# Head projections of a linear attention: from float32 matmuls of head pairs to bf16 matmuls over exact pieces

## The chip, the cores and the metric

The kernel runs on one core of one Trainium2 chip. The metric is the device time of one execution in microseconds (us). The engines named here are TensorE (PE: matmuls; PEld: its weight loads), VectorE (DVE), ScalarE (ACT), GpSimd (POOL) and SyncE (SP), which issues all DMAs of this kernel.

## The reference, cut to what matters

A block of three layers over x of shape (16, 256, 128): an attention with random features, a small FFN with fp4-rounded weights and inputs, and a state-space mixer with an FFN behind it. The change touches only the projection inside the attention's features:

```
def _compute_features(z, omega, quad_nodes, quad_weights):     # z is q or k
    zn = z / jnp.maximum(jnp.linalg.norm(z, axis=-1, keepdims=True), 1e-12)
    proj = jnp.einsum('bhtd,rhdm->rbhtm', zn, omega)   # 16 heads, d = 8, 2 nodes x 32 features
    poly = proj ** 2 * inv_sqrt_m
    exp_arg = jnp.clip(proj * sqrt_2s - s, -20.0, 20.0)
    prf = jnp.exp(exp_arg) * inv_sqrt_m
    return poly * prf * sqw                            # 64 features a head
# attention: scores = qf . kf, causal, times v, divided by its own sum
```

Each head has 8 channels for q and 8 for k, and every token of every head gets 64 projected values.

## The kernel before

The 16 sequences are worked in 8 groups of 2 (512 tokens). The program is unrolled into 10 turns, and in turn i three groups are in flight: `new` (group i) is in attention, `mid` (group i-1) in the first FFN and the front of the mixer, `old` (group i-2) in the mixer's scan and the last FFN. Turn 0 has only `new`, turns 8 and 9 have none. Each turn is written for each engine as two loops of 16 slots, and every engine works its own list strictly in order, held only by semaphores:

- Loop A, slots k = 0 to 15. For `old`, one state of the scan a slot: ACT makes the decay (L716) and the drive (L728), PE turns the drive (L1476), DVE scans (L1159), POOL multiplies with a row of C (`read_out`, L624), PE adds the states up in PSUM (`sum_states`, L1492; state 14 at the end of the loop, state 15 after the first scores of loop B). For `new`: norm, qkv, the norm of each head, and at k = 12 and 13 on PE the turned q and k of sequence b = 0 and 1, into bank 3 of PSUM (L1587). For `mid`: the first FFN, its last matmuls (`down`) at k = 14.
- Loop B, slots 0 to 15, one slot for each pair of heads of each sequence of `new`: `project` (L1417), on ACT exp and square (L704, L707), on POOL a clip (L665; DVE does it for slots 0 to 2), on DVE the product of the two (`features`, L1148), on PE the scores (L1428, L1430), on DVE and ACT their masked copy (L1169, L737), on PE the context two slots later (L1454). Between them lie the mixer's front for `mid` and the last FFN for `old`.

The projection as it was: ACT copies bank 3 to `znt` (L822, float32, at k = 13 and 14), with all 16 heads x 8 channels on the 128 partitions. `omega` lies in SBUF as 128 x 8 pairs x 128, zero except in the rows of the pair's two heads, so one float32 matmul of 128 rows, 128 columns and 512 moving columns (q and k, 256 tokens each) gives the pair's 2 x 64 features in bank 0. The compiler makes two TensorE instructions of it. There is a single bank for it: `project(s)` waits for the square of slot s-1.

PE issues `project(0)` at k = 14 of loop A, `project(1)` at its end, `project(2)` in slot 0 of loop B and then `project(k + 2)` in slot k. The SP queue is in order too. In a turn it loads C rows 4 to 15 of `old` (each once its buffer is free), stores the C rows of `mid` to DRAM when ACT has written `xdbl` in loop B (`store_c`), loads the first four of them, and stores the output.

After loop A, POOL computes the deviation for the mixer's norm (L552 to L567), and ACT normalises with it (`xn_b`) behind the features of slots 0 and 1.

## Time and profile before

| | |
|---|---|
| median of 3 runs | 1375.67 us (1375.54 to 1377.26) |
| the profiled execution | 1378.12 us |
| its span, first to last instruction | 1376.4 us |
| mean granted TensorE clock | 0.910 |
| busy: PE, DVE, ACT, POOL | 82%, 72%, 68%, 35% of the span |
| matmuls of the projection | 256 instructions, 145.8 us of PE |
| first `project` of turns 0 to 4 | 33.0, 136.3, 276.0, 428.7, 580.2 us |
| last `project` | 1109.2 us |

The times in the timeline are from the span's start. Busy shares are shares of the whole span, and the turns differ: turn 0 has attention alone, turns 2 to 7 have everything, turns 8 and 9 have no attention. A granted clock of 1.00 is 2.4 GHz, 0.50 is 1.2 GHz.

### The profile page before, as it was taken

The page shows a single profiled execution, that of the slowest core. Times are in us where ns is not written, and L with a number is a line of the kernel's source. Part 1 is how long each engine was busy: PE and PEld are TensorE (multiplying, and loading weights), DVE is VectorE, ACT ScalarE, POOL GpSimd, SP SyncE. Part 2 cuts the span into 40 slices and gives each one's busy share as a digit, 9 for nine tenths or more (in the row PEclk, how much of TensorE's full clock was granted, in tenths as well). Part 3 has the DMA queues.
Part 4 walks back from the last instruction along what each step waited for, and adds up shares of the span by engine and source line. Part 5 has one row for each costly group of instructions (what it writes and reads, how often), then busy time and mean ns, then how long its engine had stood idle before and what let it go on. Part 6 is the DMA issues. An engine that isn't in the chain of part 4 may idle for free. (4 is left out here: it accounts for less than half of the span.)

```text
span 1376.4 us, 17231 instructions
## 1 busy us (share of the span) xinstructions
PE 1126.2 (82%) x5421; PEld 621.8 (45%) x5421; DVE 985.4 (72%) x1472; ACT 937.2 (68%) x1829; POOL 484.4 (35%) x457
## 2 busy tenths in 40 slices
PE   3875887899789988899789988999889987747844
PEld 1343344544544454545544454545544454415423
DVE  1645559886897689876897689877897688645733
ACT  3543779677885769576885869586886768467711
POOL 3110216531454116621454126511543126405623
PEclk8986899999999999999999999999999999967865
DMA  2000002100110002100120102100110002001200
GB/s 73 1 8 0 19 14 62 39 1 32 41 60 9 32 1 77 31 2 31 46 54 8 33 10 68 31 24 10 48 53 1 32 24 61 17 31 38 62 0 8
DMA packets 31403, 41.12 MB, mean 30 GB/s; under 512 B 4617, under 2 KB 14674, under 8 KB 31314
## 3 DMA queue, kind: packets, MB, share of 16 engines
q1 hardware_dynamic: 31314, 40.02, 10.0%
q8 instruction: 46, 0.75, 0.2%
q14 instruction: 43, 0.35, 0.1%
HBM read 37.65 MB, written 2.36 MB: 29 GB/s over the span
## 5 line engine op out<-in xcount | busy, mean ns | idle before, releaser
L624 POOL TENSOR_TENSOR read<-state,c_row 128x1024 f32<-128x1024 f32 x128 | 300.4, 2358 | 237.7 <-DVE state L1159 68.5
L1159 DVE TENSOR_TENSOR_SCAN state<-decay,bank 128x512 f32<-128x512 f32 x256 | 295.7, 1203 | 57.5 <-PE bank L1476 48.0
L1492 PE MATMUL bank<-read,ident 128*128 128x512 f32 x512 | 258.7, 634 | 1.1 <-POOL read L624 1.1
L1476 PE MATMUL bank<-ident,drive_by_token 128*128 128x128 f32 x1024 | 161.6, 294 | 95.7 <-DVE state L1159 85.6
L728 ACT ACTIVATE drive_by_token<-dtu_t,b_t 128x256 f32<-128x256 f32 x512 | 217.3, 500 | 1.0 <-PE bank L1476 0.9
L665 POOL TENSOR_SCALAR expf<-expf 128x512 f32<-128x512 f32 x104 | 69.2, 665 | 379.6 <-ACT expf L704 379.0
L1476 PEld LDWEIGHTS bank<-ident,drive_by_token 128*128 128x128 f32 x1024 | 119.5, 148 | 162.3 <-issue 104.8
L716 ACT ACTIVATE decay<-dt,neg_a 128x510 f32<-128x510 f32 x256 | 169.7, 714 | 16.4 <-DVE state L1159 16.3
L1169 DVE TENSOR_TENSOR s_sb<-bank,causal 128x512 f32<-128x512 f32 x128 | 88.2, 689 | 112.5 <-PE bank L1430 112.5
L1417 PE MATMUL bank<-znt,omega 128*128 128x512 f32 x256 | 145.8, 653 | 10.2 <-ACT sqf L707 10.2
L704 ACT ACTIVATE expf<-bank,minus_s,root2s 128x512 f32<-128x512 f32 x128 | 99.3, 776 | 69.2 <-PE bank L1417 66.0
L1492 PEld LDWEIGHTS bank<-read,ident 128*128 128x128 f32 x512 | 97.8, 208 | 86.1 <-issue 80.1
L1454 PE MATMUL bank<-s_sb,vext 128*32 128x256 f32 (+1 forms) x1024 | 130.7, 344 | 3.2 <-ACT s_sb L737 2.9
L1428 PE MATMUL bank<-feat 64*128 64x256 f32 x512 | 96.0, 439 | 12.5 <-ACT s_sb L737 11.8
L737 ACT ACTIVATE s_sb<-bank 128x256 f32<-128x256 f32 x128 | 48.8, 381 | 76.7 <-DVE s_sb L1169 76.5
L1148 DVE SCALAR_TENSOR_TENSOR feat<-expf,scale_f,sqf 128x512 f32<-128x512 f32 x128 | 95.3, 744 | 7.0 <-POOL expf L665 4.4
L1454 PEld LDWEIGHTS bank<-s_sb,vext 128*32 128x32 f32 x1024 | 39.7, 109 | 98.4 <-issue 62.0
L1428 PEld LDWEIGHTS bank<-feat 64*128 64x128 f32 x512 | 43.6, 192 | 75.8 <-issue 61.5
L707 ACT ACTIVATE sqf<-bank 128x512 f32<-128x512 f32 x128 | 75.5, 589 | 0.0
L1417 PEld LDWEIGHTS bank<-znt,omega 128*128 128x128 f32 x256 | 44.8, 202 | 47.2 <-issue 42.1
L1430 PEld LDWEIGHTS bank<-feat 64*128 64x128 f32 x512 | 55.7, 193 | 4.1
L1430 PE MATMUL bank<-feat 64*128 64x128 f32 x512 | 54.4, 276 | 0.0
(236 smaller groups left out, 1694.6 us busy)
## 6 DMA issues: line engine op xcount, KB each, us to landing
c_row<-c_rows SPq DMA_DIRECT2D x128, 256.0 KB, 3.2
xa<-x_dram SPq DMA_DIRECT2D x8, 256.0 KB, 3.6
out_dram<-x SPq DMA_DIRECT2D x8, 256.0 KB, 2.3
omega<-omega_t_dram SPq DMA_DIRECT2D x1, 512.0 KB
c_rows<-xdbl SPq DMA_DIRECT2D x8, 32.0 KB, 1.6
wqkv<-w_qkv_t_dram SPq DMA_DIRECT2D x1, 192.0 KB
state<-w_down_dram SPq DMA_DIRECT2D x1, 176.0 KB, 2.5
state<-w_gate_dram SPq DMA_DIRECT2D x1, 128.0 KB, 2.0
```

The lines of the kernel that those rows point to most:

```text
L624: pool.tensor_tensor(read[:, s % STATE_BUFFERS], state[:, s % STATE_BUFFERS], c_row[:, s % C_BUFFERS].unsqueeze(1).broadcast_to([P, DT, TO ...
L704: act.activation(expf[:, s % 2], bank[:, 0], ACT.Exp, bias=minus_s[:], scale=root2s[:]).then_inc(exp_done.sem, 1)
L716: last = act.activation(decay[:, s % 2, k, :, 1:], dt[:, k].rearrange("p (b t) -> p b t", b=SEQS)[:, :, 1:], ACT.Exp, scale=neg_a[:, k, s: ...
L728: last = act.activation(by_token[:, s % DRIVES, t], dtu_t[:, t], ACT.Identity, scale=b_t[:, t, s:s + 1])
L1148: dve.scalar_tensor_tensor(feat[:, s % 2], expf[:, s % 2], scale_f[:], sqf[:, s % 2], ALU.mult, ALU.mult).then_inc(feat_done.sem, 1)
L1159: dve.tensor_tensor_scan(state[:, s % STATE_BUFFERS, c], decay[:, s % 2, c].rearrange("p b t -> p (b t)"), bank[:, DRIVE_BANK + c], 0.0, A ...
L1417: pe.matmul(bank[:, 0], omega[:, j], znt[:, b], start=True, stop=True).then_inc(proj_ps.sem, 1)
L1428: pe.matmul(bank[:, 1 + h, 0:SEQ], f[:, SEQ:SEQ + P], f[:, 0:SEQ], start=True, stop=True)
L1430: last = pe.matmul(bank[:, 1 + h, SEQ:SEQ + P], f[:, SEQ + P:], f[:, P:SEQ], start=True, stop=True)
L1454: last = pe.matmul(o, columns, scored, start=(k == 0 and below == 0), stop=(k == 1 and below == 1))
L1476: last = pe.transpose(bank[:, DRIVE_BANK + c, t * P:(t + 1) * P], by_token[:, s % DRIVES, t, c * P:(c + 1) * P], ident[:])
L1492: last = pe.matmul(bank[:, 6 + k], ident[:], read[:, s % STATE_BUFFERS, k], start=(s == 0), stop=(s == STATES - 1))
```

## The change

Each float32 value of z and of omega is split into three bf16 values (high, middle, low) whose sum is the value. The product of a head is then the sum of nine products of 8 channels, and these are stacked on 3 x 3 x 8 = 72 rows of one bf16 matmul: rows (i, d, j) hold piece i of z and piece j of omega. So a slot has two matmuls, one a head, each of 72 rows, 64 columns and 512 moving columns, into the lower and the upper half of bank 0.

What is new for each sequence: ACT writes the high piece from bank 3 (in the place of the copy to `znt`), DVE subtracts it (`z_left`), ACT rounds that to the middle piece (one slot later, so behind the high piece of the other sequence), POOL subtracts again and has the low piece (`z_lowest`, before `read_out` of slots 14 and 15). SP stores the three pieces to DRAM and loads, for each head, the 24 rows of it, each repeated on three partitions; a slot has one of 4 buffers. DVE splits omega in turn 0 (five operations on 72 x 1024), and it also goes through DRAM once. `project(0)` and `project(1)` now stand at the end of loop A, behind the sum of state 14. Some pairs of semaphores were merged, with the same order of work.

```
+            def store_z(group, b):
+                for i, piece in enumerate((z_high, z_mid, z_low)):
+                    sp.wait_ge(piece.sem, piece.at(group, b + 1))
+                    sp.dma_start(z_dram[b, :, i], z_part[:, b, i]).then_inc(z_stored.sem, 16)
+            def load_z(group, s):
+                b, j = divmod(s, PAIRS)
+                sp.wait_ge(z_stored.sem, z_stored.at(group, PIECES * (b + 1)))
+                sp.wait_ge(proj_ps.sem, proj_ps.at(group, s + 1 - Z_BUFFERS))
+                for half, h in enumerate(heads_of(j)):
+                    sp.dma_start(
+                        z_row[:, s % Z_BUFFERS, half],
+                        z_dram[b, h].rearrange("i d t -> (i d) t").unsqueeze(1).broadcast_to(
+                            [PIECES * HD, PIECES, 2 * SEQ])).then_inc(
+                                z_loaded[s % Z_BUFFERS].sem, 16)
...
+                if turn.has_new:
+                    store_z(turn.new, 0)
+                    for s in range(Z_BUFFERS):
+                        load_z(turn.new, s)
+                    store_z(turn.new, 1)
+                    for s in range(Z_BUFFERS, 12):
+                        load_z(turn.new, s)
                 if turn.has_mid:
                     store_c(turn.mid)
                     for s in range(C_BUFFERS):
                         load_c(turn.mid, s)
+                if turn.has_new:
+                    for s in range(12, SLOTS):
+                        load_z(turn.new, s)
...
+            def z_lowest(group, b):
+                pool.wait_ge(z_mid.sem, z_mid.at(group, b + 1))
+                pool.tensor_tensor(z_part[:, b, 2], z_left[:], z_part[:, b, 1], ALU.subtract
+                                   ).then_inc(z_low.sem, 1)
             def body(turn):
                 for k in range(SLOTS):
+                    if turn.has_new and k in (14, 15):
+                        z_lowest(turn.new, k - 14)
                     attention_rest(turn, k)
                     if turn.has_old:
                         read_out(turn, k)
...
                     act.wait_ge(znt_ps.sem, znt_ps.at(new, b + 1))
-                    act.activation(
-                        znt[:, b], bank[:, 3].rearrange("p (k t) -> p k t", k=2), ACT.Copy
-                    ).then_inc(znt_done.sem, 1)
+                    act.wait_ge(z_stored.sem, z_stored.at(new, PIECES * (b + 1 - SEQS)))
+                    act.activation(z_part[:, b, 0], bank[:, 3], ACT.Copy).then_inc(z_high.sem, 1)
+                if turn.has_new and k in (14, 15):
+                    b = k - 14
+                    act.wait_ge(z_rest.sem, z_rest.at(new, b + 1))
+                    act.activation(z_part[:, b, 1], z_left[:], ACT.Copy).then_inc(z_mid.sem, 1)
...
+                if turn.is_first and k == 1:
+                    split_omega()
+                if turn.has_new and k in (13, 14):
+                    b = k - 13
+                    dve.wait_ge(z_high.sem, z_high.at(new, b + 1))
+                    dve.wait_ge(z_low.sem, z_low.at(new, b))
+                    dve.tensor_tensor(z_left[:], bank[:, 3], z_part[:, b, 0], ALU.subtract
+                                      ).then_inc(z_rest.sem, 1)
...
             def project(ga, s):
-                b, j = divmod(s, PAIRS)
-                pe.wait_ge(znt_done.sem, znt_done.at(ga, b + 1))
+                loaded_row = z_loaded[s % Z_BUFFERS]
+                pe.wait_ge(loaded_row.sem, loaded_row.at(ga, 2 * (s // Z_BUFFERS + 1)))
                 pe.wait_ge(sq_done.sem, sq_done.at(ga, s))
-                pe.matmul(bank[:, 0], omega[:, j], znt[:, b], start=True, stop=True).then_inc(
-                    proj_ps.sem, 1)
+                for half, h in enumerate(heads_of(s % PAIRS)):
+                    last = pe.matmul(bank[PH * half:PH * (half + 1), 0], omega[:, h],
+                                     z_row[:, s % Z_BUFFERS, half], start=True, stop=True)
+                last.then_inc(proj_ps.sem, 1)
...
-                    pe.wait_ge(znt_done.sem, znt_done.at(new, b))
+                    pe.wait_ge(z_rest.sem, z_rest.at(new, b))
...
                     if turn.has_mid and k == 14:
+                        if turn.has_new:
+                            pe.wait_ge(z_rest.sem, z_rest.at(new, SEQS))
                         down(ffn_a, mid, 1)
-                    if turn.has_new and k == 14:
-                        project(new, 0)
                     if turn.has_old:
                         for s in SUMS[k]:
                             sum_states(old, s)
                     attention_rest(turn, k)
-                if turn.has_new:
-                    project(new, 1)
                 if turn.has_old:
                     sum_states(old, STATES - 2)
+                if turn.is_first:
+                    pe.wait_ge(omega_moved, 32)
+                if turn.has_new:
+                    project(new, 0)
+                    project(new, 1)
```

## Rows read from the trace of the kernel before

**Rows 1.** Groups of instructions: busy us, mean ns of one, idle before it.

```profile
L1417 PE MATMUL bank<-znt,omega 128*128 128x512 f32 x256 | 145.8, 653 | 10.2 <-ACT sqf L707 10.2
...
L704 ACT ACTIVATE expf<-bank,minus_s,root2s 128x512 f32<-128x512 f32 x128 | 99.3, 776 | 69.2 <-PE bank L1417 66.0
...
L1169 DVE TENSOR_TENSOR s_sb<-bank,causal 128x512 f32<-128x512 f32 x128 | 88.2, 689 | 112.5 <-PE bank L1430 112.5
...
L707 ACT ACTIVATE sqf<-bank 128x512 f32<-128x512 f32 x128 | 75.5, 589 | 0.0
```

**Rows 2.** Windows of turn 4, loop B; PE, PEld, DVE, ACT, POOL busy (instructions), clock, DMA.

```profile
595.00:618.00 23.00, 21.95 (x115) 9.73 (x114) 20.36 (x39) 19.05 (x36) 4.67 (x9) 0.99 0.01 2
618.00:648.00 30.00, 28.41 (x152) 14.71 (x150) 18.88 (x27) 20.60 (x35) 4.25 (x6) 0.89 0.12 36
```

**Rows 3.** The same two windows, the instructions of the projection (L1417) alone: PE, PEld.

```profile
595.00:618.00 23.00, 5.32 (x10) 1.66 (x10) 0.99 0.01 2
618.00:648.00 30.00, 7.20 (x12) 2.28 (x12) 0.89 0.12 36
```

**Rows 4.** Timeline of PE, a slot of loop B in turn 4: start, us.

```profile
605.12 1.02 PE L1417 MATMUL bank<-znt,omega 128*128 128x512 f32 x2
606.08 0.62 PE L1454 MATMUL bank<-s_sb,vext 128*32 128x256 f32 x4
606.63 0.71 PE L1428 MATMUL bank<-feat 64*128 64x256 f32 x4
...
607.84 1.12 PE L1417 MATMUL bank<-znt,omega 128*128 128x512 f32 x2
```

**Rows 5.** Timeline of PE between loop A and loop B in turn 4.

```profile
576.56 0.60 PE L1587 MATMUL bank<-ident,qk 128*128 128x128 f32 x4
...
580.21 1.02 PE L1417 MATMUL bank<-znt,omega 128*128 128x512 f32 x2
...
585.45 0.71 PE L1428 MATMUL bank<-feat 64*128 64x256 f32 x4
...
588.68 0.63 PE L1409 MATMUL bank<-ident,xn_b 128*128 128x128 f32 x4 [0.38 <-ACT xn_b L692]
```

**Rows 6.** Timeline of POOL over the same stretch.

```profile
570.56 6.96 POOL L624 TENSOR_TENSOR read<-state,c_row 128x1024 f32<-128x1024 f32 x3 [2.83 <-DVE a_ffn_h L1127]
580.79 2.35 POOL L624 TENSOR_TENSOR read<-state,c_row 128x1024 f32<-128x1024 f32 x1 [3.27 <-DVE state L1159]
...
586.50 0.35 POOL L567 TENSOR_TENSOR b_ln_shift<-b_ln_shift,b_ln_rstd 128x4 f32<-128x4 f32 x2
```

**Rows 7.** Timeline of turn 0, all engines.

```profile
24.00 1.26 POOL L641 TENSOR_TENSOR xab<-xa,bout 128x512 f32<-128x512 f32 x1 [11.92 <-DMA wglu<-glu_w_t_dram]
...
30.22 1.08 PE L1587 MATMUL bank<-ident,qk 128*128 128x128 f32 x4 [8.77 <-DVE qk L1231]
31.34 0.60 ACT L822 ACTIVATE znt<-bank 128x512 f32<-128x512 f32 x1 [4.03 <-PE bank L1587]
...
32.97 1.92 PE L1417 MATMUL bank<-znt,omega 128*128 128x512 f32 x2
```

**Rows 8.** DMA issues: count, KB each, us from issue to landing.

```profile
c_row<-c_rows SPq DMA_DIRECT2D x128, 256.0 KB, 3.2
...
c_rows<-xdbl SPq DMA_DIRECT2D x8, 32.0 KB, 1.6
```

**Rows 9.** Timeline of the SP queue: start, us of the issue.

```profile
16.70 0.43 SPq L455 DMA_DIRECT2D wmix<-mix_out_t_dram  x1
```

**Rows 10.** Windows of turns 0 and 1, loop B, columns as in rows 2.

```profile
33.00:90.00 57.00, 49.49 (x306) 23.72 (x305) 33.18 (x54) 29.18 (x56) 8.79 (x13) 0.93 0.01 1
136.00:206.00 70.00, 61.18 (x346) 29.20 (x346) 37.97 (x63) 50.37 (x95) 11.93 (x20) 0.92 0.06 16
```

**Rows 11.** Windows of turn 4 where the granted clock falls, columns as in rows 2.

```profile
612.00:618.00 6.00, 4.95 (x27) 2.17 (x26) 5.86 (x11) 4.35 (x11) 0.96 (x2) 0.97 0.03 7
618.00:624.00 6.00, 6.00 (x16) 2.30 (x16) 0.67 (x1) 4.48 (x9) 0.61 (x1) 0.50 0.56 175
```

More of the change, by code:

```diff
@@ L39 @@
 CROWS, CTILE, CPITCH = 16, 32, 48
+PIECES = 3
+ROWS = PIECES * PIECES * HD
+Z_BUFFERS = 4
 CHUNKS = SEQ // P
@@ L137, in build @@
         bout = sb("bout", [P, C])
-        omega = sb("omega", [P, PAIRS, P])
+        omega = sb("omega_pieces", [ROWS, HEADS, PH], BF16)
         node = sb("node", [P, 1])
@@ L175, in build @@
         vext = sb("vext", [P, TILES, HEADS, CPITCH])
-        znt = sb("znt", [P, SEQS, 2, SEQ])
+        z_part = sb("z_pieces", [P, SEQS, PIECES, 2 * SEQ], BF16)
+        z_row = sb("z_rows", [ROWS, Z_BUFFERS, 2, 2 * SEQ], BF16)
         expf = sb("expf", [P, 2, 2 * SEQ])
@@ L183, in build @@
         ctx_t = sb("ctx_t", [P, 2 * SEQ])
+        z_left = ctx_t
+        omega_all = feat[0:ROWS].rearrange("p k t -> p (k t)")
+        omega_left = expf[0:ROWS].rearrange("p k t -> p (k t)")
+        omega_part = s_sb[0:ROWS].rearrange("p k h t -> p (k h t)")[
+            :, 0:PIECES * HEADS * PH // 2].bitcast(BF16).rearrange(
+                "p (i c) -> p i c", i=PIECES)
         rden = sb("rden", [P, CHUNKS * HEADS])
@@ L341, in build @@
         znt_ps = events("a_znt_in_psum", SEQS)
-        znt_done = events("a_znt", SEQS)
+        z_high = events("a_z_high", SEQS)
+        z_rest = events("a_z_rest", SEQS)
+        z_mid = events("a_z_mid", SEQS)
+        z_low = events("a_z_low", SEQS)
+        z_stored = events("a_z_in_dram", SEQS * PIECES, 16)
+        z_loaded = [events(f"a_z_rows_{j}", 2 * SLOTS // Z_BUFFERS, 16) for j in range(Z_BUFFERS)]
         proj_ps = events("a_proj_in_psum", SLOTS)
@@ L428, in _ @@
             sp.dma_start(wqkv[:], w_qkv_t).then_inc(attention_loaded, 16)
[L429 removed]
+            sp.dma_start(bqkv, b_qkv).then_inc(attention_loaded, 16)
             sp.dma_start(node[:], nodes).then_inc(attention_loaded, 16)
             sp.dma_start(scale_f[:], weights).then_inc(attention_loaded, 16)
[L432 removed]
+            sp.dma_start(omega_all, omega_t).then_inc(attention_loaded, 16)
             for e in every_event:
@@ L548, in deviation @@
             def deviation(norm, group):
-                pool.wait_ge(norm.var.sem, norm.var.at(group, 1))
+                pool.wait_ge(norm.var.sem, norm.var.at(group, 2))
                 mean, var = norm.mean_var[:, :, 0], norm.mean_var[:, :, 1]
@@ L689, in normalise @@
             def normalise(norm, group, src, dst, layer=0):
-                act.wait_ge(norm.dev.sem, norm.dev.at(group, 1))
+                act.wait_ge(norm.dev.sem, norm.dev.at(group, 3))
                 for t in range(TILES):
@@ L767, in h_magic @@
                 act.activation(f.quant_h.magic, f.h[pair][:].rearrange("p t n -> p (t n)"),
-                               ACT.Abs, scale=LIFT).then_inc(f.h_magic.sem, 1)
+                               ACT.Abs, scale=LIFT).then_inc(f.magic.sem, 1)
             def ffn_ht(f, group, pair):
@@ L1024, in statistics @@
                     last = dve.bn_stats(norm.stats[:, t], src[:, t])
-                last.then_inc(norm.counted.sem, 1)
-                dve.wait_ge(norm.counted.sem, norm.counted.at(group, 1))
+                last.then_inc(norm.var.sem, 1)
+                dve.wait_ge(norm.var.sem, norm.var.at(group, 1))
                 for t in range(TILES):
@@ L1116, in hidden_lifted @@
             def hidden_lifted(f, group, pair):
-                dve.wait_ge(f.h_magic.sem, f.h_magic.at(group, pair + 1))
+                dve.wait_ge(f.magic.sem, f.magic.at(group, pair + 2))
                 lift(f.quant_h, hidden(f, pair)).then_inc(f.h_lifted.sem, 1)
@@ L1403, in _ @@
             pe.matmul(bank[:, 7, 0:3 * C], minus_part[:], wqkv[:], start=True, stop=False)
-            pe.matmul(bank[:, 7, 0:3 * C], part[:], bqkv[:], start=False, stop=True
+            pe.matmul(bank[:, 7, 0:3 * C], part[:], bqkv, start=False, stop=True
                       ).then_inc(bias_spread, 1)
@@ L1813, in head_pairs @@
         t = omega.transpose(1, 2, 0, 3).reshape(HEADS, HD, PH)
-        laid = np.zeros((HEADS, HD, PAIRS, 2, PH), omega.dtype)
-        for j in range(PAIRS):
-            for half, h in enumerate(heads_of(j)):
-                laid[h, :, j, half] = t[h]
-        return laid.reshape(HEADS * HD, PAIRS, 2 * PH)
+        rows = np.repeat(t.transpose(1, 0, 2).reshape(HD, HEADS * PH), PIECES, axis=0)
+        return np.tile(rows, (PIECES, 1))
     def columns(v):
```

52 lines of the change are left out of this document (35 added, 17 removed).

## The prediction

> **What bounds the kernel now.** I read the groups of instructions first, then the timelines of one slot and of the place between the loops, then the windows. The reader is to see in the groups that the projection is 256 TensorE instructions of 0.65 us, and that ACT has 0.78 + 0.59 us of exp and square behind each pair of them [rows 1]. The timeline of a slot shows the pace: after a projection starts, the context starts 0.96 us later, and the next projection after 2.72 us, with no idle mark on any PE line; PE is the engine that this slot waits for [rows 4]. The windows say how long this holds in turn 4, one of the six full turns (2 to 7). From 595 to 618 us PE is busy 21.95 of 23 us, but DVE 20.36 and ACT 19.05 too: three engines are near their limit. From 618 to 648 PE has 28.41 of 30, DVE only 18.88 and ACT 20.60: there PE alone sets the pace [rows 2]. The projection is 5 pairs of instructions (5.32 us) of the first and 6 pairs (7.20 us) of the second [rows 3]. Turns 0 and 1 are the clearest case, PE 49.49 of 57 and 61.18 of 70 us [rows 10]. So a cheaper projection pays in loop B, by less than its own busy time.
>
> Between the loops another chain counts. POOL finishes the product of state 15 at 583.14, works out the deviation until 586.85 [rows 6], and PE can turn the normalised tiles only at 588.68 [rows 5]. Whatever delays POOL's last two products delays the mixer's front of that turn.
>
> **The price of the new matmul.** No bf16 matmul is in the trace. From above: two instructions at the price of the two float32 ones, 0.96 us, a gain of nothing; from below 0. The nearest row is the context: four instructions of 256 columns on different column tiles, two heads, take 0.55 us (606.08 to 606.63) [rows 4]. Two of 512 columns on two column halves stream as many columns. That would be 0.55 us; since a float32 instruction does more work a column than a bf16 one should, I take 0.5, which saves 0.5 us a slot of PE (0.96 to 1.05 before).
>
> The Trainium skill ("TensorE: Matmul & The Clock Gate", "Back-to-back issue gap") puts a bf16 matmul of 512 columns at 216 ns from start to start at the full clock, and its part on row and column tiling lets column tiles run at once: an estimate of 0.43 us or of some 0.22 for the pair. By the first the total below would be about 2 us lower; the second is the first rival. No run here shows it yet.
>
> **What it brings in loop B of a full turn.** 595 to 618: 5 x 0.5 = 2.5 us of PE, but DVE leaves only 23 - 20.36 = 2.64 us, and part of that waits on ACT and POOL; I credit half, 1.3. 618 to 648: 6 x 0.5, plus 0.5 because one of the six runs at the half clock (7.20 us for six against 5.32 for five, so about 1.9 for that one [rows 3]), 3.5 us, and DVE has 11 us free: 3.3. The other three of the fourteen stand in the ramp and the tail: 1.5 us, of which I credit 0.9. Sum 5.5 us.
>
> **What it costs between the loops, full turn.** I follow turn 4. PE turns sequence 1 at 576.56, done 577.16 [rows 5]. The high piece of sequence 1 (ACT 0.6, as the copy to `znt` [rows 7]) ends at 577.8, and only behind it, in ACT's order, comes the middle piece of sequence 0, to 578.4. `z_lowest(0)` on POOL then: nearest is the 128x512 addition of 1.26 us [rows 7], above it half a `read_out` (6.96 / 3 / 2 = 1.16) [rows 6]; I take 1.2, to 579.6. Queued behind it is `read_out(14)`, which ended at 577.5 before; now it runs 579.6 to 581.95. `z_lowest(1)` follows to 583.15, then `read_out(15)` to 585.5 instead of 583.14: 2.35 us late. The deviation, the normalisation and the tiles at 588.68 come as much later, about 591.0. DVE: `z_left` of sequence 1 waits for POOL's 579.6 and takes 0.69 (the mask, also read from PSUM [rows 1]), so the scan of state 15 ends near 582.6, before POOL wants it. PE's `down` waits for that 580.3; 1.5 us idle. The extra DVE 2 x 0.7 and ACT 2 x 0.6 us lie in waits of these engines here.
>
> Does the data reach `project(0)`? The low piece is there at 579.6. A store of 128 KB is between the 32 KB that landed after 1.6 us and the 256 KB after 3.2 [rows 8]; the loads of 72 KB likewise, two of them, 0.43 us apart on SP [rows 9]. With 2.0 and 2.0 the row is there at 584.1, before PE has summed state 14 (about 585.4). `project(0)` is then 5 us later than the 580.21 of before, but the scores, at 585.45 before, come at 585.4 + 0.5 + 0.8 exp + 0.5 clip + 0.75 product = 588.1 or so: 2.65 us late and near the same delay, and the transposes of `xn_b` follow at 591.0. The cost is 2.35 us.
>
> PE now has several idle pieces of 1 to 1.5 us in a place that was full. The granted clock fell after a stretch with PE at 4.95 of 6 us, and the next 6 us ran at 0.50 [rows 11]. I count half of such a stretch more, 3 us at 1.2 GHz, at 1 us of path.
>
> Full turn: 2.35 + 1 - 5.5 = -2.15 us, times six -12.9.
>
> **Turns 0 and 1.** Turn 1: 15 x 0.5 = 7.5 us, times PE's share 61.18 / 70 [rows 10], 6.5; the entry costs 2, the clock 1: -3.5. Turn 0 has nothing to hide the round trip. The first copy ends at 31.94 [rows 7]; then `z_left` 0.7, PE's second transposes 1.1, high 0.6, middle 0.6, low 1.26, store 2.0, second load 0.43 + 1.6: `project(0)` at about 40.3 instead of 32.97, +7.3. Its slots save 14 x 0.5 = 7, but DVE rounds weights in nine of them (33.18 of 57 us busy in all [rows 10]); I credit 5.5. Net +1.8. Splitting omega (five operations, 5 to 6 us of DVE) lies between the norm and the sums of squares, where DVE waits, and its round trip ends long before 40 us.
>
> **SP.** In loop B each slot issues two loads, 0.86 us of SP, and a row may be loaded when the projection four slots earlier is done, 11 us at 2.72 a slot, against 0.43 + 3.2 at worst. `store_c` stands behind the load for slot 11, which needs `project(7)`, issued before `xdbl` is made; the four C rows (1 MB) then go ahead of slot 12's row, with some three slots in hand. Cost nothing; if that cover is gone, slots 12 to 15 wait.
>
> **Sum.** -12.9 - 3.5 + 1.8 = -14.6 us. The profiled execution took 1378.12 us, 1.72 around its span of 1376.4; it would be 1363.5. Against the median 1375.67 it gives 1361.
>
> **The rivals.**
> - PE is the whole pace and the halves overlap (pair 0.25, saving 0.75): 14 x 0.75 = 10.5, credited 9.5, less 2.35, is -7.2 a full turn, -43; turns 0 and 1 -2 and -9. About 1322. For it: no idle on PE lines in the slot [rows 4]. Against: DVE at 20.36 of 23 [rows 2].
> - DVE and ACT set the pace as soon as PE gives way: only the stretch from 618 pays, 2.4 us, which the entry takes: about 1376. For it: the same 20.36 and 19.05.
> - The granted clock, and this one ends slower. The projection was the densest work of the slot, 128 x 128 tiles; what stays are the context's and the scores' small tiles, and PE idles more. Where PE was at 4.95 of 6 us the clock fell to 0.50 for the next 6 [rows 11]. If each loop B has 10 us more of that, PE does 5 us less work in it, times eight is +40: 1361 + 40 = 1401. It decides from 14.6 / 8 = 1.8 us a turn, 3.7 us more at 1.2 GHz. Against: turn 0 keeps a mean of 0.93 [rows 10]. The Trainium skill ("TensorE: Matmul & The Clock Gate", on how the clock gate oscillates) has the clock follow how busy PE has been; rows 11 agree in so far as the fall comes behind idle pieces, but PE was at 83% there.
> - The pair costs what the float32 pair did, 0.96: nothing is saved, and 6 x 3.35 + 3 + 7.3 = +30: 1406. Slower, too.
> - The rows come late. With 3.2 us a transfer [rows 8] `project(0)` moves 2.4 us, less 1.3 in hand; with PE at the entry late by about 2 us in each of eight turns, 1377.
>
> **How the numbers follow.** Chances: forecast 0.43 (1348 to 1373), overlap 0.13, DVE and ACT 0.14, clock 0.18, no cheaper 0.05, late rows 0.07. Faster by over 0.2% (2.8 us, about what a measurement of this kernel can tell from no change): 0.43 + 0.13, and 0.03 each of the second and third rival, 0.62. Same: 0.06 of the second, 0.02 of late rows, 0.08. Slower: 0.30. The range from 1320 to 1398 leaves out the last two hundredths of the overlap, the no-cheaper case and half of the clock case, together 0.16 to 0.2.
>
> **What the profile after would show.** Right: the two instructions of the projection 0.2 to 0.3 us apart, the slot's pace in turn 0 down from 2.8 towards 2.3 us; POOL's `read_out` of state 15 2.4 us behind the transposes of sequence 1 compared with before; turns 2 to 7 some 2 us shorter; `project(0)` of turn 0 near 40 us, released by a DMA. Wrong: a mean clock under 0.88; idle of PE in front of the projection put down to DMA in slots above 4; a projection that keeps PE for 0.9 us; DVE over 90% in loop B with PE at 75%. The most fragile terms are the credits of rows 2 and the clock.

## The result, and the profile after

The changed kernel took 1398.9 us (median of 4, 1396.6 to 1409.28) against 1376.47 of the kernel before in the same session: a ratio of 1.0172 (95%: 1.0117 to 1.0227). It is 1.7% slower; 1361 was forecast, 1398 was the top of the range. The profiled execution is the slowest of the four (1409.28, 10 us above their median), so its pieces add up to more than the median's difference. The granted clock is the first thing to see, the new kernel above the old one:

```profile
core 0: 1407.5 us, clock 0.872
```

```profile
core 0: 1376.4 us, clock 0.910
```

The clock has two levels, 1.2 and 2.4 GHz, so a mean of 0.872 says that 1407.5 x 2 x 0.128 = 360 us ran at 1.2 GHz, against 248 before. The three unprofiled runs had 0.876 to 0.880. The prediction had named a mean clock under 0.88 as a sign of being wrong. The groups of instructions of after, to read beside [rows 1], say that the matmul itself became at least as cheap as forecast:

```profile
L1506 PE MATMUL bank<-z_rows,omega_pieces 72*64 72x512 bf16 x256 | 57.2, 437 | 38.8 <-ACT sqf L767 28.4
...
L1518 PE MATMUL bank<-feat 64*128 64x256 f32 x512 | 108.5, 477 | 27.8 <-ACT s_sb L797 24.3
```

PE's time in the projection fell from 145.8 to 57.2 us. It now waits 38.8 us in front of it (10.2 before), mostly for the square on ACT, which frees bank 0. A slot of loop B in turn 4, PE's timeline, against [rows 4]:

```profile
622.12 0.41 PE L1506 MATMUL bank<-z_rows,omega_pieces 72*64 72x512 bf16 x2
622.45 0.63 PE L1544 MATMUL bank<-s_sb,vext 128*32 128x256 f32 x4
623.01 0.71 PE L1518 MATMUL bank<-feat 64*128 64x256 f32 x4
...
624.82 0.41 PE L1506 MATMUL bank<-z_rows,omega_pieces 72*64 72x512 bf16 x2 [0.54 <-ACT sqf L767]
```

The context follows 0.33 us after the projection instead of 0.96: 0.63 us saved. But the last line starts only after an idle 0.54 us.

I cut both traces at the first transposes of `att` of each turn. The whole difference between the two profiled executions (31 us) can be placed with that:

| us | before | after | forecast of the difference | measured |
|---|---|---|---|---|
| turn 0 | 90.2 | 93.5 | +1.8 | +3.3 |
| turn 1 | 116.3 | 116.9 | -3.5 | +0.6 |
| turns 2 to 7 | 920.9 | 947.1 | -12.9 | +26.2 |
| the rest | 249 | 250 | 0 | +1 |

These are the marks themselves, before and then after: the ends of turns 0, 1 and 7.

```profile
90.25 0.66 PE L1409 MATMUL bank<-ident,att 128*128 128x128 f32 x4 [1.13 <-DVE att L1184]
...
206.54 0.66 PE L1409 MATMUL bank<-ident,att 128*128 128x128 f32 x4 [0.26 <-DVE att L1184]
...
1127.48 0.60 PE L1409 MATMUL bank<-ident,att 128*128 128x128 f32 x4
```

```profile
93.52 0.65 PE L1497 MATMUL bank<-ident,att 128*128 128x128 f32 x4 [1.13 <-DVE att L1263]
...
210.45 0.66 PE L1497 MATMUL bank<-ident,att 128*128 128x128 f32 x4 [0.26 <-DVE att L1263]
...
1157.54 0.60 PE L1497 MATMUL bank<-ident,att 128*128 128x128 f32 x4
```

Inside the full turns, loop A gave back 0.7 us a turn and the entry (from the first transposes of q and k to the mixer's first projection, `xp`) took 3.8 us more on average. Loop B, which was to give 5.5 us, gave nothing and took 1.3 us more on average: 75.2 to 78.1 us, where before had 73.7 to 76.9. In turn 4, from `xp` to the transposes, windows of before and after (columns as in [rows 2]):

```profile
590.20:667.00 76.80, 70.63 (x394) 37.68 (x395) 56.59 (x98) 56.45 (x104) 10.66 (x20) 0.93 0.05 15
```

```profile
608.60:684.60 76.00, 67.67 (x394) 37.52 (x395) 55.52 (x96) 56.42 (x104) 10.63 (x17) 0.87 0.12 36
...
629.00:642.00 13.00, 11.17 (x46) 5.44 (x48) 6.63 (x12) 9.66 (x20) 1.89 (x3) 0.61 0.34 103
```

PE has 3 us less work, counted at a lower clock: 0.87 against 0.93. The last line is 13 us out of it at 0.61, with PE busy 86% of the time.

### The profile page after: what moved, and what is told of

Read it like the earlier page. It is cut to its first block and busy times, and to the rows that moved or that the text cites. A ratio compares the mean times of both kernels' runs of the same rounds, so it can differ in the third digit from the quotient of the medians.

```text
span 1407.5 us, 17744 instructions
## 1 busy us (share of the span) xinstructions
PE 1096.2 (78%) x5421; PEld 621.4 (44%) x5421; DVE 991.3 (70%) x1493; ACT 943.4 (67%) x1845; POOL 502.4 (36%) x473
## 5 line engine op out<-in xcount | busy, mean ns | idle before, releaser
L1544 PE MATMUL bank<-s_sb,vext 128*32 128x256 f32 (+1 forms) x1024 | 142.7, 374 | 1.8 <-ACT s_sb L797 0.9
L1518 PE MATMUL bank<-feat 64*128 64x256 f32 x512 | 108.5, 477 | 27.8 <-ACT s_sb L797 24.3
L1518 PEld LDWEIGHTS bank<-feat 64*128 64x128 f32 x512 | 50.5, 208 | 87.3 <-issue 73.3
L1506 PE MATMUL bank<-z_rows,omega_pieces 72*64 72x512 bf16 x256 | 57.2, 437 | 38.8 <-ACT sqf L767 28.4
L1520 PEld LDWEIGHTS bank<-feat 64*128 64x128 f32 x512 | 65.8, 216 | 5.0
L1544 PEld LDWEIGHTS bank<-s_sb,vext 128*32 128x32 f32 x1024 | 42.7, 116 | 52.4 <-issue 35.1
L1520 PE MATMUL bank<-feat 64*128 64x128 f32 x512 | 63.1, 300 | 0.0
L1506 PEld LDWEIGHTS bank<-z_rows,omega_pieces 72*64 72x64 bf16 x256 | 15.7, 110 | 96.6 <-issue 75.1
```

What stands on the lines that cost most here:

```text
L1518: pe.matmul(bank[:, 1 + h, 0:SEQ], f[:, SEQ:SEQ + P], f[:, 0:SEQ], start=True, stop=True)
L1520: last = pe.matmul(bank[:, 1 + h, SEQ:SEQ + P], f[:, SEQ + P:], f[:, P:SEQ], start=True, stop=True)
L1544: last = pe.matmul(o, columns, scored, start=(k == 0 and below == 0), stop=(k == 1 and below == 1))
```

## The experiments

"Ratio" is to the kernel before on the same chip. The time at 1.2 GHz is 2 x time x (1 - clock), the mean over the runs of a kernel.

| kernel | ratio (95%) | median us | us at 1.2 GHz |
|---|---|---|---|
| before | 1 | 1373.0 to 1377.2 | 238 to 246 |
| after | 1.0172 (1.0117 to 1.0227) | 1398.9 | 345 |
| e1_one_piece | 1.0022 (0.9992 to 1.0052) | 1375.58 | 328 |
| e2_filler | 1.0352 (1.0301 to 1.0402) | 1424.48 | 276 |
| e3_late_float32 | 1.0043 (1.0009 to 1.0076) | 1380.0 | 231 |
| e4_two_buffers | 1.0208 (1.016 to 1.0255) | 1403.43 | 354 |
| e5_no_dram | 1.0001 (0.9967 to 1.0035) | 1373.25 | 285 |
| e6_one_piece_warm | 0.9903 (0.987 to 0.9937) | 1360.46 | 250 |
| e7_one_piece_light | 0.9787 (0.9758 to 0.9815) | 1344.72 | 290 |
| e8_before_light | 0.9939 (0.991 to 0.9967) | 1367.33 | 240 |
| e9_warm | 1.0077 (1.0047 to 1.0107) | 1385.05 | 262 |
| e10_three_products | 0.9894 (0.9875 to 0.9914) | 1361.06 | 245 |
| e11_traffic | 1.0011 (0.9987 to 1.0035) | 1377.64 | 291 |
| e12_traffic_waited | 1.0030 (0.9996 to 1.0063) | 1381.86 | 295 |
| e13_wide | 1.0196 (1.017 to 1.0222) | 1404.86 | 330 |
| e14_column_halves | 1.0039 (1.0011 to 1.0067) | 1382.44 | 296 |
| e15_72_rows | 1.0146 (1.0095 to 1.0197) | 1393.45 | 330 |
| e16_128_rows | 1.0047 (1.0021 to 1.0073) | 1382.28 | 294 |

(A single run of e11_traffic of 1938 us, at a clock of 1.0, stands outside its ratio and its mean. What made it is not known.)

**e1_one_piece.** Before, with the cheap matmul alone, at its old place:

```
+        omega_b = sb("omega_bf16", [P, PAIRS, P], BF16)
-        znt = sb("znt", [P, SEQS, 2, SEQ])
+        znt = sb("znt", [P, SEQS, 2, SEQ], BF16)
...
-                pe.matmul(bank[:, 0], omega[:, j], znt[:, b], start=True, stop=True).then_inc(
+                pe.matmul(bank[:, 0], omega_b[:, j], znt[:, b], start=True, stop=True).then_inc(
```

> The kernel before with only the matmul made cheap: znt and omega rounded once to bf16 (so the projection has bf16 precision, the two lower pieces and seven of the nine products are left out), one 128x128x512 bf16 matmul a slot in the old places, no DMA, no pieces. If PE sets the pace of loop B, some 0.7 us x 14 slots x 8 turns come off less a part: 1320 to 1345. If DVE and ACT take over the pace at once, 1370 to 1378 with the mean granted clock at about 0.91. If the clock takes it back, loop B gets more stretches at 0.50, the mean clock falls below 0.89, and the time is 1365 to 1385.

1.0022: the price of the projection can fall with nothing else changed, and the kernel doesn't get faster. What was lost isn't only in the entry. The clock fell from 0.910 to 0.885:

```profile
core 0: 1367.8 us, clock 0.885
```

**e2_filler.** After, with useless float32 work in front of each pair, to bring PE's load back:

```
             def project(ga, s):
...
+                pe.matmul(bank[:, 0, 0:3 * C], ident[:], wqkv[:], start=True, stop=True)
```

> The changed kernel with a float32 matmul of 384 columns (0.7 us) put in front of each pair, into the same bank, its result overwritten: PE has its old load back. If PE sets the pace at a full clock, 0.7 us x 14 x 8 x 0.7 is +55 us: 1450. If DVE and ACT set it, within 5 us of the 1399 of the changed kernel or up to 20 above. If the clock took the gain, the fillers restore it: mean clock over 0.90, and the time at 1399 or below it.

It was far too much work, and it stands in turns 0 and 1 too (103.6 and 129.1 us against 93.5 and 116.9). 1.0352 doesn't decide between the theories by itself. But the time at 1.2 GHz fell from 345 to 276 us, and the six full turns took 943.5 us with 96 fillers of 384 columns in them, against the 947.1 of the profiled after. That run of after was 10 us above its median and this one 3, so the fillers cost a few us there and not nothing; but it is little for so much work, and it asked for the finer dose of e6 and e9.

**e3_late_float32.** Before, with `project(0)` and `project(1)` at the late place:

```
-                    if turn.has_new and k == 14:
-                        project(new, 0)
...
-                if turn.has_new:
-                    project(new, 1)
                 if turn.has_old:
                     sum_states(old, STATES - 2)
...
+                if turn.has_new:
+                    project(new, 0)
+                    project(new, 1)
```

> The kernel before with only project(0) and project(1) moved behind the sum of state 14, float32 as they were. If the entry costs by its order alone, it is slower by 2 to 4 us in each of seven turns: 1390 to 1405. If the entry's cost comes from POOL's two subtractions and the clock, within 5 us of before, for the deviation on POOL still ends last.

1.0043: the later place costs about 0.4%, 6 us, and by itself lowers no clock (231 us at 1.2 GHz).

**e4_two_buffers.** After, with a `z_left` for each sequence, so that nothing of DVE waits for POOL's first subtraction, and both subtractions behind `read_out(14)`:

```
-        z_left = ctx_t
+        z_left = feat
...
-                    if turn.has_new and k in (14, 15):
-                        z_lowest(turn.new, k - 14)
+                    if turn.has_new and k == 15:
+                        z_lowest(turn.new, 0)
+                        z_lowest(turn.new, 1)
...
-                    dve.wait_ge(z_low.sem, z_low.at(new, b))
...
+                    dve.wait_ge(z_low.sem, z_low.at(turn.new, SEQS))
```

> The changed kernel with a buffer of z_left for each sequence (in the idle feature buffers), so that DVE doesn't wait for POOL before the scan of state 15, and with both low pieces behind read_out(14). If the entry costs by the wait of DVE and POOL's order, about 2 us in each full turn come back: 1383 to 1389. If the entry's cost is the late rows and the clock, under 4 us: 1395 to 1399.

1.0208, no faster than after. The deviation is ready 2.1 us sooner in turn 4: POOL's last product of it now ends 9.7 us after the second transposes of q and k started (591.86), 11.8 in after. But the next wait was right behind, the row out of DRAM (PE, then POOL):

```profile
600.31 0.41 PE L1507 MATMUL bank<-z_rows,omega_pieces 72*64 72x512 bf16 x2 [0.84 <-DMA z_rows<-z_in_dram]
...
601.24 0.35 POOL L619 TENSOR_TENSOR b_ln_shift<-b_ln_shift,b_ln_rstd 128x4 f32<-128x4 f32 x2
```

ACT normalises only behind the features of slots 0 and 1. In turn 4 the entry still became 2.1 us shorter, but over the six full turns it averages 23.9 us against 24.1 in after, so what POOL gained did not last. The order on POOL, to which the prediction gave the whole price of the entry but for 1 us, isn't alone in it.

**e5_no_dram.** After, with the chain of pieces on ACT, DVE and POOL and the late place kept, but no transfers, and one matmul over the high pieces where they lie:

```
-                loaded_row = z_loaded[s % Z_BUFFERS]
-                pe.wait_ge(loaded_row.sem, loaded_row.at(ga, 2 * (s // Z_BUFFERS + 1)))
+                b, j = divmod(s, PAIRS)
+                pe.wait_ge(z_low.sem, z_low.at(ga, b + 1))
...
+                pe.matmul(bank[:, 0], omega_b[:, j], z_part[:, b, 0], start=True, stop=True).then_inc(
+                    proj_ps.sem, 1)
```

> The changed kernel without its DMAs of z and omega: the pieces are made as they are, but the projection is one bf16 matmul of the high pieces of a pair (128 x 128), at the end of loop A, so seven of nine products are left out. If the round trip through DRAM sets the entry, 2 us or more a turn come back and turn 0 is 5 us shorter: 1380 or less. If POOL's order and the clock set it, 1390 to 1399 but for turn 0.

1.0001. The 1.7% goes with what e5 took away: the traffic and its waits, or the shape of the matmul.

**e6_one_piece_warm.** e1 with useless float32 work of 256 columns before the projections from slot 3 on, in turns with `old`:

```
+                if warm:
+                    pe.matmul(bank[:, 0, 0:256], ident[:], wqkv[:, 0:256], start=True, stop=True)
```

> The one-piece kernel with a float32 matmul of 256 columns (0.5 us) in front of each projection from slot 3 on in turns 2 to 9. Turns 0 and 1 and all entries keep their cheap matmul. If the clock takes the gain of the cheap matmul in the full turns, this work costs nothing: loop B (from the first matmul of the mixer to the next turn's first transposes) stays at 73 to 76 us and the granted clock in it rises to over 0.95. If the cheap matmul's time is needed, loop B gets longer by 13 x 0.5 x 0.7 = 4 us or more in each full turn, +25 in all.

0.9903 against the 1.0022 of e1, with disjoint intervals. More work on PE, a higher clock, a shorter kernel:

```profile
core 0: 1364.9 us, clock 0.905
```

**e7_one_piece_light and e8_before_light.** e1, and before, with exp, square and the product cut to 256 of 512 columns:

```
-                act.activation(sqf[:, s % 2], bank[:, 0], ACT.Square).then_inc(sq_done.sem, 1)
+                act.activation(sqf[:, s % 2, 0:SEQ], bank[:, 0, 0:SEQ], ACT.Square).then_inc(sq_done.sem, 1)
```

> The one-piece kernel with exp, square and their product on 256 of the 512 columns (the other half of the features isn't computed), so ACT does some 0.54 us and DVE some 0.3 us less in each slot. If these two engines and the chain from projection through exp and square set the pace of loop B once PE gives way, 14 x 0.5 x 6 and more come off: 1320 to 1340. If PE's clock is what holds it, little changes, under 10 us.

> The kernel before with the same halves left out. If PE alone set the pace before, nothing changes: 1366 to 1376. If ACT and DVE were already part of the pace, it gains as much as the one-piece kernel does from the same cut.

The same cut is worth 2.35% behind the cheap matmul and 0.6% in before, so ACT and DVE hold the kernel more once PE gives way. Loop B of the full turns says the same when it is compared at an equal granted clock: with light features it took 73.1 us against 73.7 to 74.1 in before (clock 0.98), and 72.2 to 72.8 against 74.4 to 74.9 in e1 (clock 0.91). That the six full turns as a whole took 903.8 us in e7 and 904.2 in e8 fits with the clock: 290 us at 1.2 GHz against 240.

**e9_warm.** After with fillers as in e6, and two more between the loops:

```
+                            pe.matmul(bank[:, 2, 0:HID], ident[:], wqkv[:, 0:HID], start=True,
+                                      stop=True)
...
+                    if turn.has_mid:
+                        pe.matmul(bank[:, 1, 0:3 * C], ident[:], wqkv[:], start=True, stop=True)
...
-                            project(new, k + 2)
+                            project(new, k + 2, turn.has_old)
```

> The changed kernel, whole, with useless float32 matmuls: 256 columns (0.5 us) in front of the pair from slot 3 on in turns 2 to 9, 352 columns where PE waits for z_left at the end of loop A, 384 between project(0) and project(1). If the clock's theory holds for the changed kernel as it did for the one-piece one (-1.2%), 1375 to 1388, with a mean clock over 0.89. If the changed kernel is held by its rows and not by the clock, the added work costs 0 to 20 us: 1399 to 1420.

1.0077 against 1.0172, with disjoint intervals too: over half of the loss came back by adding work.

```profile
core 0: 1382.3 us, clock 0.907
```

**e10_three_products.** High and middle pieces only, three of the nine products. The pieces stay where ACT and DVE write them (128 rows), three accumulating matmuls a slot, at the old places, no POOL step and no transfer:

```
+                pe.matmul(bank[:, 0], omega_b[:, 1, j], znt[:, b, 0], start=True, stop=False)
+                pe.matmul(bank[:, 0], omega_b[:, 0, j], znt[:, b, 1], start=False, stop=False)
+                pe.matmul(bank[:, 0], omega_b[:, 0, j], znt[:, b, 0], start=False, stop=True).then_inc(
```

> Another way to the cheap projection: high and middle piece of z and of omega stay in SBUF in the old 128-row layout, and three bf16 matmuls of 128x128x512 (high x high, high x middle, middle x high) add up in bank 0, in the old places; the smaller products are left out. No DMA, one subtraction on DVE a sequence. PE has some 0.65 us a slot, between the one-piece kernel and before. If the clock is kept by dense work, as with the filler, it is faster than before by 0.5 to 1%: 1360 to 1368. If only float32 work keeps it, as the one-piece kernel: 1370 to 1380.

0.9894: faster than both kernels. It has three matmuls where e1 has one, and its ratio is 1.3% lower, with 245 us at 1.2 GHz instead of 328. It differs from e1 in one subtraction a sequence as well, which can only cost. PE in turn 4:

```profile
601.63 0.39 PE L1429 MATMUL bank<-znt,omega_bf 128*128 128x512 bf16 x1
601.86 0.38 PE L1430 MATMUL bank<-znt,omega_bf 128*128 128x512 bf16 x1
602.07 0.38 PE L1431 MATMUL bank<-znt,omega_bf 128*128 128x512 bf16 x1
602.38 0.63 PE L1468 MATMUL bank<-s_sb,vext 128*32 128x256 f32 x4
```

0.75 us from the first to the context, against 0.96 of float32 and 0.33 of after.

**e11_traffic and e12_traffic_waited.** e5 with all stores and loads running again; in e12 each projection also waits for its row, though it doesn't read it:

```
+                loaded_row = z_loaded[s % Z_BUFFERS]
+                pe.wait_ge(loaded_row.sem, loaded_row.at(ga, 2 * (s // Z_BUFFERS + 1)))
```

> The kernel without DRAM in the path (high pieces only, one matmul a slot), but the stores and loads of the z rows run as in the changed kernel; nothing but SP waits for them. If the traffic itself costs (SP's issues, C rows delayed, contention), it goes from 1.000 of before towards 1.017. If only the waiting for the rows costs, it stays at 1.000 of before, within 0.3%.

> The run before (traffic, high pieces only, one 128x128 matmul a slot) with one thing more: each projection waits until its rows have been loaded, as in the changed kernel; it doesn't read them. What is left between it and the changed kernel is the form of the matmul (two of 72 rows and 64 columns). If the waiting for rows costs the 1.6% between them, it comes to 1.013 to 1.019 of before. If the small tiles do, by the clock, it stays below 1.005.

1.0011 and 1.0030. Against e5 the traffic comes to 0.1% and the wait to 0.2% more, with errors of some 0.4% each, so neither can be told from nothing. The profiled runs show where the wait lies: turn 0 took 87.6 us in e11 and 93.1 in e12. What remained was the shape: two matmuls of 72 rows and 64 columns against one of 128 and 128.

**e13_wide and e14_column_halves.** The columns, from both sides: after with weights of 128 columns, zero for the other head, accumulated; and e12 with its matmul cut into two halves of columns.

```
-                    last = pe.matmul(bank[PH * half:PH * (half + 1), 0], omega[:, h],
-                                     z_row[:, s % Z_BUFFERS, half], start=True, stop=True)
+                    last = pe.matmul(bank[:, 0], omega_wide[:, h].rearrange("p x c -> p (x c)"),
+                                     z_row[:, s % Z_BUFFERS, half], start=(half == 0),
+                                     stop=(half == 1))
```

```
+                for half in range(2):
+                    last = pe.matmul(bank[PH * half:PH * (half + 1), 0],
+                                     omega_b[:, j, PH * half:PH * (half + 1)], z_part[:, b, 0],
+                                     start=True, stop=True)
```

> The changed kernel, whole, with the two column halves made full: each head's weights lie in 128 columns with zeros in the other half, and the two 72x128x512 matmuls add up in bank 0. The array's columns are all in use, and PE needs about twice the time of the overlapping pair (some 0.2 us more a slot, 25 us of work in all). If the narrow tiles take the granted clock down, and with it the 1.4% between the changed kernel and the last run, the time falls towards 1.003 of before, mean clock about 0.90. If something else of the changed kernel costs, it stays at 1.017 or goes above.

> The mirror: the last run (rows waited for, high pieces only), its 128x128 matmul cut into two of 128 rows and 64 columns, one to each half of bank 0. They overlap, so PE's time stays about the same. If narrow tiles take the clock down, 1.012 to 1.018 of before with a mean clock below 0.885; if it is not the tiles, it stays at 1.003.

1.0196 beside 1.0172, and 1.0039 beside 1.0030. Neither the width of the tile nor one matmul or two makes the loss. e14 says it more cleanly: e13 also has more work on PE, and its turn 0 is 3.0 us longer, where its weights are spread over 128 columns.

**e15_72_rows and e16_128_rows.** The rows, from both sides: e12 with its matmul on 72 of the 128 rows, so with less work in it; and after, the full nine products, with the rows of `omega` and of `z_rows` filled up with zeros to 128.

```
-                pe.matmul(bank[:, 0], omega_b[:, j], z_part[:, b, 0], start=True, stop=True).then_inc(
+                pe.matmul(bank[:, 0], omega_b[0:ROWS, j], z_part[0:ROWS, b, 0], start=True, stop=True).then_inc(
```

```
-        omega = sb("omega_pieces", [ROWS, HEADS, PH], BF16)
+        omega = sb("omega_pieces", [P, HEADS, PH], BF16)
...
-        z_row = sb("z_rows", [ROWS, Z_BUFFERS, 2, 2 * SEQ], BF16)
+        z_row = sb("z_rows", [P, Z_BUFFERS, 2, 2 * SEQ], BF16)
...
+            dve.memset(omega[64:P], 0.0).then_inc(cleared, 1)
+            dve.memset(z_row[64:P], 0.0).then_inc(cleared, 1)
```

> The kernel with the rows waited for and one matmul a slot on the high pieces, but on 72 of the 128 rows only (the products of the other rows are left out), all 128 columns. PE's time stays. If the clock looks at how many rows of the array are used, the full turns get longer by 4 to 5 us each and it comes to 1.012 to 1.018 of before with a mean clock below 0.885. If not, 1.003.

> The changed kernel, whole, with omega and the z rows filled up to 128 partitions with zeros, so that the pair is 128 rows by 64 columns; the DMAs still write 72 rows. Nothing else changes. If the number of rows is what takes the clock, it falls from 1.017 to 1.003 to 1.006 of before and the mean clock rises to about 0.90. If not, it stays at 1.017.

Both moved, in the expected directions, and the intervals are disjoint: 72 rows took e12 from 1.0030 to 1.0146, 128 rows took after from 1.0172 to 1.0047. 345 us at 1.2 GHz became 294. The instruction that does it, in e16, is as long as that of after:

```profile
625.59 0.41 PE L1509 MATMUL bank<-z_rows,omega_pieces 128*64 128x512 bf16 x2
```

The profiled runs of e15 and e16, in this order, against 0.900 in e12 and 0.872 in after:

```profile
core 0: 1388.0 us, clock 0.884
```

```profile
core 0: 1383.7 us, clock 0.889
```

**Loop B at an equal clock.** In the profiled runs loop B of a full turn (from the first record of `xp` to the next transposes of `att`) goes with its own granted clock. Before took 73.7 to 74.1 us where the clock was 0.98 and 76.3 to 76.9 where it was 0.93. The whole new projection on 128 rows (e16) took 70.4 at 0.98 and 73.6 at 0.93, and e5 70.5 and 73.1. After never had more than 0.89. Turn 3 in before, e16 and after, columns as in [rows 2]:

```profile
438.70:512.83 74.13, 67.53 (x394) 35.67 (x395) 56.25 (x96) 56.45 (x104) 10.15 (x17) 0.98 0.05 16
```

```profile
442.91:513.32 70.41, 60.18 (x394) 33.12 (x395) 55.97 (x97) 55.92 (x104) 10.61 (x17) 0.98 0.12 39
```

```profile
451.52:527.55 76.03, 67.71 (x394) 37.46 (x395) 55.50 (x96) 56.38 (x104) 10.63 (x17) 0.87 0.12 36
```

So at an equal clock the cheap projection is worth some 3 to 3.5 us of loop B a turn, and the lower clock of after takes that away, as it does in the turns of e16 at 0.89 (75.7 and 76.7 us). A turn at 0.98 and one at 0.93 stand 2.6 (before) and 3.2 us (e16) apart: 0.33 to 0.43 us for each us more at 1.2 GHz, an estimate, as the clock has two digits here.

**What a us at 1.2 GHz costs.** Runs of one and the same kernel differ in clock and time together. Lines through the runs of one kernel, time against time at 1.2 GHz, rise by 0.26 to 0.41 us per us for before (six sets of 13 to 19 runs: 0.26 to 0.36) and for e1, e3, e5, e12, e14 and e16 (10 runs each); e11, with nine, gives 0.16, and the sets of 4 to 7 runs scatter from -0.06 (e10) to 0.45 (e2). By 0.35, the 51 us between after and e16 are worth 18 us (their ratios to before differ by 1.25%, 17 us), and the 35 us between e15 and e12 are worth 12 (1.16%, 16 us). So the clock accounts for most of what the rows cost, and for all of it within the errors of these ratios. Between after and before lie about 104 us at 1.2 GHz: 36 us of time (27 to 43 by the ends of the slopes). The means differ by 24 us in their own session and by 26 over all sets of before, so the rest of the change brought about -10 us, and anything from -1 to -19 by the ends. This is a correlation inside each kernel that is used across kernels, so the 36 and the -10 are estimates.

## Why the prediction was wrong, by its own steps

**Where it failed: the credit for loop B of a full turn, -5.5 us.** The time that PE saved there (3 us less busy in turn 4, at a lower clock) bought nothing at the clock that was left; loop B of the profiled run stands 0.8 us under before in turn 4 and 1.3 us over it in the mean of the full turns. At an equal clock it would have been worth 3 to 3.5 us, so the credit was some 2 us a turn too large even so. But it was made from rows at the clock of before, and the price of the clock's fall was put at 1 us a turn and at the entry; this term is the one that failed. That was 7 us in all (six full turns and turn 1 had 1 us each); with about 104 us more at 1.2 GHz it was 36, by the estimate above. Without the clock the forecast's other terms sum to -14.6 - 7 = -21.6, and the estimate leaves -10 (-1 to -19): the other terms probably had the right sign and were too large, and the size of the fall of the clock was missing.

**The price of the matmul: cheaper than taken.** 0.33 us to the context against 0.5 taken, so 0.63 us saved where 0.5 was forecast; 256 instructions at two a slot. In turn 0, where the float32 pace was 2.81 us (48.23 to 51.04), slots come at 2.31, as forecast:

```profile
60.05 0.41 PE L1506 MATMUL bank<-z_rows,omega_pieces 72*64 72x512 bf16 x2
62.37 0.41 PE L1506 MATMUL bank<-z_rows,omega_pieces 72*64 72x512 bf16 x2
64.68 0.41 PE L1506 MATMUL bank<-z_rows,omega_pieces 72*64 72x512 bf16 x2
```

The Trainium skill ("TensorE: Matmul & The Clock Gate", "Back-to-back issue gap") has a bf16 matmul of 512 columns every 216 ns, by its formula for isolated ones; the three of e10 start 0.23 and 0.21 us apart and agree.

**The entry of a full turn: +3.35 forecast, +3.8 measured, with other parts.** PE and POOL between the loops of turn 4, against [rows 5, 6]:

```profile
591.27 0.60 PE L1677 MATMUL bank<-ident,qk 128*128 128x128 f32 x4
595.10 1.60 PE L1627 MATMUL bank<-wdown,a_ffn_ht 128*128 128x128 f32 x12 [1.71 <-DVE ctx_t L1320]
...
600.08 0.41 PE L1506 MATMUL bank<-z_rows,omega_pieces 72*64 72x512 bf16 x2
601.93 0.41 PE L1506 MATMUL bank<-z_rows,omega_pieces 72*64 72x512 bf16 x2 [1.45 <-ACT sqf L767]
602.74 0.80 PE L1518 MATMUL bank<-feat 64*128 64x256 f32 x4 [0.40 <-DVE feat L1227]
603.70 3.22 PE L1582 MATMUL bank<-read,ident 128*128 128x512 f32 x4
606.71 1.06 PE L1497 MATMUL bank<-ident,xn_b 128*128 128x128 f32 x4
```

```profile
593.10 1.15 POOL L723 TENSOR_TENSOR z_pieces<-ctx_t,z_pieces 128x512 bf16<-128x512 f32 x1 [3.15 <-ACT z_pieces L888]
594.21 2.36 POOL L676 TENSOR_TENSOR read<-state,c_row 128x1024 f32<-128x1024 f32 x1
596.52 1.16 POOL L723 TENSOR_TENSOR z_pieces<-ctx_t,z_pieces 128x512 bf16<-128x512 f32 x1
597.63 2.35 POOL L676 TENSOR_TENSOR read<-state,c_row 128x1024 f32<-128x1024 f32 x1
602.75 0.35 POOL L619 TENSOR_TENSOR b_ln_shift<-b_ln_shift,b_ln_rstd 128x4 f32<-128x4 f32 x2
```

The order on POOL came as worked out, 1.15 us a subtraction, and the product of state 15 started 2.1 us later against those transposes, but the end of the deviation moved by 1.5 us only, 11.83 us behind the second transposes (10.29 before), not 2.35. PE's transposes of `xn_b` came 3.3 us later on the same scale (606.71 - 591.27 = 15.44 against 12.12). In front of them stands the sum of state 15, here 3.22 us at the lower clock; before it took 1.98:

```profile
586.31 1.98 PE L1492 MATMUL bank<-read,ident 128*128 128x512 f32 x4
```

So the clock is also in the entry. e3 and e4 fit with that: the late place alone costs 0.4%, and POOL's delay taken away brings nothing to the whole.

**Turn 0: +1.8 forecast, +3.3 measured.** `project(0)` started at 41.51 instead of the forecast 40.3 (PE waited 7.94 us), and its first seven projections ran at the half clock: the stretch at 1.2 GHz that begins at 24 us goes on to 58 us, to 41 before. That took part of what the slots saved. The wait for the rows is 5.6 us of turn 0 by the profiled runs of e11 and e12.

**Turn 1: -3.5 forecast, +0.6 measured.** `project(0)` came 50.1 us behind the mark that begins the turn, 46.1 before: 4.0 us later, where 2 was forecast. The rest goes with the clock again. Windows of the turn, before and then after, columns as in [rows 2]:

```profile
90.25:206.54 116.29, 88.85 (x433) 46.92 (x433) 62.41 (x112) 68.30 (x130) 18.65 (x33) 0.82 0.04 12
```

```profile
93.52:210.45 116.93, 81.16 (x432) 45.65 (x433) 63.68 (x114) 68.73 (x132) 21.21 (x35) 0.77 0.13 39
```

PE has 7.7 us less busy time in it, at a clock of 0.77 instead of 0.82, and the turn is no shorter.

**SP: right, though the issue was dearer.** A load of a row takes 0.76 us of SP, not 0.43:

```profile
L519 SPq DMA_DIRECT2D z_rows<-z_in_dram x256: 755/759/1226, 38.2 to 1118.8; - x128
```

A transfer of a row ended the idle time of 15 pairs of weight loads, one in turn 0 and two in each turn after it. They are those of the first two projections of a turn, so no slot further on waited; in turn 4:

```profile
600.07 0.11 PEld L1506 LDWEIGHTS bank<-z_rows,omega_pieces 72*64 72x64 bf16 x2 [0.76 <-DMA z_rows<-z_in_dram]
601.90 0.14 PEld L1506 LDWEIGHTS bank<-z_rows,omega_pieces 72*64 72x64 bf16 x2 [1.72 <-DMA z_rows<-z_in_dram]
```

Against before, e11 bounds what the traffic costs at 0.35% and e12 what traffic and wait cost at 0.63% (both have the cheaper matmul too, so part of a cost could be covered by its saving; against e5 the two come to 0.3%, with an error of 0.5%).

**The rivals.** The clock one had 0.18 and the price 1401. The time landed near that price, and that the clock is the cause is shown by e6, e9, e15 and e16, but its mechanism as stated is not: it blamed the small tiles of context and scores and PE's idle time. e15 changes neither and does less work in nothing but the projection, with 56 rows left out. The projection's own rows were taken for harmless. DVE and ACT as the pace (0.14) is shown in part by e7 against e8: lighter features are worth four times as much behind the cheap matmul, and about twice as much in loop B of the full turns at an equal clock. They are a part of the pace and not the whole of it. Halves that overlap: in the slot the pair goes by in 0.33 us, between that rival's 0.25 and the forecast, and the full turns gained nothing by it. No cheaper: false by the slot. Late rows: in turn 0, e12; in the other turns at most a small part.

**What stays open.** Why a matmul on 72 rows, as long and as frequent as one on 128, brings the clock down; e1 has 128 rows and still 328 us at 1.2 GHz, more than e5 (285), whose projections come later. So the rows are one cause of several.

## What to carry to other kernels

Price an edit of PE's work at the clock that will be left, not at the clock of the trace: 1 us more at 1.2 GHz went with 0.26 to 0.41 us here, and a cheaper matmul bought with fewer array rows gave more than its saving back. Filling the rows up with zeros took most of the loss away (1.0172 to 1.0047) but did not make the change a gain. Before packing operands on fewer than 128 partitions, time it with the other rows at zero, which takes a few lines. When an operand can stay where it was written, compare three plain products on all rows (e10, 1.1% faster than before) with one packed product behind a chain of subtractions and transfers (1.7% slower).

## What the runs showed of the hardware

- Rows of the array and the clock: on 72 instead of 128 rows the kernel had 345 instead of 294 us at 1.2 GHz, and 330 instead of 295 in e15 against e12. Rows of zeros counted like others (294 us in e16, 295 and 296 in e12 and e14). 64 or 128 columns made no difference of over 0.3% to the time (e13, e14).
- Useless matmuls shorten a kernel: 1.0022 to 0.9903 (e6) and 1.0172 to 1.0077 (e9). The Trainium skill ("TensorE: Matmul & The Clock Gate", Part 1, on the clock gate) has the clock follow how busy PE has lately been; these two agree. That e15, with the same number of projections of the same length as e12, falls back by 1.2% is not covered by that.
- The row's way through DRAM: 2.3 us for the store of 128 KB, 0.76 us of SP to issue each load of 72 KB, and 5.6 us in turn 0 from the end of the low piece (35.95 us) to `project(0)` (41.51).
